# The output products of a head pair dealt over two steps in the second and fourth attention

## The reference

```python
q = (x @ Wq).reshape(B, Nq, h, dh)
k = (context @ Wk).reshape(B, Nk, h, dh)
v = (context @ Wv).reshape(B, Nk, h, dh)
attn = jax.nn.softmax(jnp.einsum('bqhd,bkhd->bhqk', q, k) * scale, axis=-1)
out = jnp.einsum('bhqk,bkhd->bqhd', attn, v).reshape(B, Nq, h * dh)
return out @ Wo + bo
...
x = x + jnp.tanh(g_xattn[1]) * _L1_xattn_ref(_layernorm(x, axis=-1), ctx_768, ...)
```

## Time and profile before

| what | value |
|---|---|
| median of 3 runs | 2148.47 us (2147.4 to 2151.1) |
| profiled execution, its own time | 2147.12 us |
| its span, first to last instruction | 2145.3 us |
| mean granted TensorE clock | 0.900 |
| PE / PEld / DVE / ACT / POOL busy | 82% / 58% / 62% / 59% / 52% |
| second attention | about 347 to 608 us |
| fourth attention | about 1767 to 2028 us |

### The profile page before, as it was taken

The page is one execution under the profiler, slowest core; times in us unless marked ns, Lnnn a source line. Parts: engine busy times, 40 slices in busy tenths (PEclk is TensorE's granted clock), DMA queues, the critical chain, the costliest instruction groups (busy, mean ns, idle before and its releaser), DMA issues. The chain is left out here.

```text
span 2145.3 us, 55182 instructions
## 1 busy us (share of the span) xinstructions
PE 1769.2 (82%) x22168; PEld 1236.0 (58%) x22169; DVE 1329.7 (62%) x2556; ACT 1272.8 (59%) x1627; POOL 1109.8 (52%) x1052
## 2 busy tenths in 40 slices
PE   1699636999947769999999999999736839999778
PEld 1244325888845626666666666666535727888645
DVE  3767376888864366555555555555244547888765
ACT  3357423777734326777777777777624527777553
POOL 2100003555542337777777777777752336775534
PEclk9779858999968859999999999999957969999899
DMA  6401100000032010000000000000122111000000
GB/s 175 80 6 11 27 0 2 3 3 3 2 102 74 25 47 11 11 14 11 10 13 12 11 10 14 11 10 11 32 83 56 36 48 34 3 3 3 2 6 16
DMA packets 95263, 55.20 MB, mean 26 GB/s; under 512 B 43341, under 2 KB 88728, under 8 KB 94918
## 3 DMA queue, kind: packets, MB, share of 16 engines
q1 hardware_dynamic: 86820, 42.61, 8.2%
q0 software_dynamic: 3584, 6.36, 0.9%
q10 hardware_dynamic: 4610, 2.71, 0.5%
HBM read 30.16 MB, written 13.75 MB: 20 GB/s over the span
## 5 line engine op out<-in xcount | busy, mean ns | idle before, releaser
L1422 POOL TENSOR_TENSOR aw_p_lo<-aw_p,aw_p_hi 128x512 f16<-128x512 f32 x512 | 576.5, 1158 | 191.0 <-issue 168.8
L1438 DVE TENSOR_REDUCE aw_max_part<-ps 128x1 f32<-128x512 f32 x512 | 351.2, 690 | 289.7 <-PE ps L1244 284.9
L859 POOL TENSOR_TENSOR ap_p_lo<-ap_p,ap_p_hi 128x512 f16<-128x512 f32 x256 | 291.0, 1158 | 181.6 <-issue 173.9
L1374 ACT ACTIVATE aw_p<-ps 128x1024 f32<-128x1024 f32 x256 | 260.0, 1015 | 206.1 <-PE ps L1275 204.0
L1289 PE MATMUL ps<-ctx_hi_lo,aw_p_hi 128*128 128x97 f16 x2048 | 288.9, 206 | 2.5 <-POOL aw_p_lo L1422 2.5
L1291 PE MATMUL ps<-ctx_hi_lo,aw_p_hi 128*128 128x96 f16 x2048 | 288.0, 207 | 0.0
L1293 PE MATMUL ps<-ctx_hi_lo,aw_p_lo 128*128 128x97 f16 x2048 | 287.4, 204 | 0.0
L1381 ACT ACTIVATE aw_p_hi<-aw_p 128x1024 f16<-128x1024 f32 x256 | 270.6, 1057 | 8.1
L1291 PEld LDWEIGHTS ps<-ctx_hi_lo,aw_p_hi 128*128 128x128 f16 x2048 | 197.9, 97 | 25.2
L1289 PEld LDWEIGHTS ps<-ctx_hi_lo,aw_p_hi 128*128 128x128 f16 x2048 | 196.5, 96 | 12.1 <-POOL aw_p_lo L1422 4.7
L1293 PEld LDWEIGHTS ps<-ctx_hi_lo,aw_p_lo 128*128 128x128 f16 x2048 | 201.9, 99 | 0.0
(11 more groups left out here) (464 smaller groups left out, 4979.8 us busy)
## 6 DMA issues: line engine op xcount, KB each, us to landing
sf_weights_raw<-in_L_w SPq DMA_DIRECT2D x24, 256.0 KB, 4.2
slot_scratch<-at_empty_rows SPq DMA_DIRECT2D x16, 260.0 KB
sf_fetched<-slot_scratch SPq DMA_DIRECT2D x16, 260.0 KB, 2.9
sf_weights_raw<-in_L_w SPq DMA_DIRECT2D x8, 512.0 KB, 3.9
x_norm<-result_scratch SPq DMA_DIRECT2D x8, 256.0 KB, 4.0
aw_queries<-aw_queries SPq DMA_DIRECT2D x32, 64.0 KB, 1.9
aw_queries<-aw_q_lo SPq DMA_DIRECT2D x32, 64.0 KB, 2.0
raw<-in_L_q SPq DMA_DIRECT2D x3, 512.0 KB, 11.9
```

The costliest lines, as they stand in the source:

```text
L859: nc.gpsimd.tensor_tensor(p_lo[:, i % 2, h, :], p[:, i % 2, h, :], p_hi[:, i % 2, h, :], ALU.subtract).then_inc(lo_done, 1)
L1374: nc.scalar.activation(p[:, n % 2, :].rearrange("p (b q) -> p b q", b=2), s, ACT.Exp, scale=1.0 / QS).then_inc(exp_done, 1)
L1422: nc.gpsimd.tensor_tensor(p_lo[:, n % 4, cols], p[:, n % 2, cols], p_hi[:, n % 4, cols], ALU.subtract).then_inc(lo_done, 1)
L1438: nc.vector.tensor_reduce(mpart[:, b % 2, k:k + 1], ps[:, max_bank(b, k), :], AX.X, ALU.max).then_inc(m_done, 1)
```

## The change

`project(u)` becomes `project(u, half)`. It is called in every step instead of in every second one: in the odd step `2u + 3` with half 0 (query tiles 0 and 1, six products), in the even step `2u + 4` with half 1 (query tiles 2 and 3, six products). Its place inside the step stays, ahead of `weighted(i)`; in an even step that is behind `turn`. The semaphore `y_ready` is raised at the end of half 1 only. The waits at the head of `project` are issued in both calls. `add` goes from the odd to the next even step on VectorE, behind the low half of the turned output and ahead of `max_rows`. The list of steps has one step more at its end.

```diff
-        steps = range(-3, NH + 2)
+        steps = range(-3, NH + 3)
...
-                def project(u):
+                def project(u, half):
                     qb, pair = block_of(u)
                     cols = slice(pair * P, (pair + 1) * P)
                     pe.wait_ge(t_done, u + 1)
                     if pair == 0 and qb:
                         pe.wait_ge(y_done, qb)
-                    for t in range(TQ):
+                    for t in (2 * half, 2 * half + 1):
...
-                    ins.then_inc(y_ready, 1)
+                    if half:
+                        ins.then_inc(y_ready, 1)
...
-                    if i % 2 and is_unit((i - 3) // 2):
-                        project((i - 3) // 2)
+                    if is_unit((i - 3) // 2):
+                        project((i - 3) // 2, 1 - i % 2)
...
-                    if i % 2 and is_unit((i - 3) // 2) and (i - 3) // 2 % NP == NP - 1:
-                        add((i - 3) // 2 // NP)
+                    if i % 2 == 0 and is_unit(i // 2 - 2) and (i // 2 - 2) % NP == NP - 1:
+                        add((i // 2 - 2) // NP)
```

## The result

The changed kernel takes 2135.6 us (median of 5 runs, 2132.26 to 2138.92), the kernel before 2151.1 (5 runs beside it, 2147.4 to 2152.76): ratio 0.9929, 95% interval 0.9912 to 0.9946, so 15 us or 0.7% faster. In a second set of runs it was 2127.74 (6 runs) against 2148.29 (11 runs): ratio 0.9913, interval 0.9887 to 0.9938. Forecast was a gain of 16.8 us, a ratio of 0.9922. The profiled execution took 2135.6 us, its span is 2133.8, and the granted clock is 0.90 as before.

The account below looks back on a forecast made before the run. TensorE bounds odd steps, VectorE even ones. Per attention 8.7 us saved by products plus 1.7, less 2.0 for the add, is 8.4; both give 16.8, so 2131.7 us, range 2128.5 to 2138.

Parts of the forecast that it names:

- What bounds each step: Both attention stretches: TensorE holds odd steps, VectorE even ones; six products leaving cut odd steps from 4.087 to 3.753 us.
- Rival B: Odd steps are not TensorE's, so only the add's move counts: 2.6 us slower, 2151.1; chance 0.03.
- The cover of the even step: Even steps: 0.39 us between TensorE's next free slot and VectorE's release hides the six added products (0.334 us).
- Rival A: Even step's cover is only 0.23 us, or the second wait costs a slot: 2137.8 us; chance 0.09, its extreme 0.02.
- The satisfied wait: Even steps: the repeated wait for the turned rest (t_done) costs nothing, at most one slot of 0.056 us.
- GpSimd and the second head: Even steps: no new TensorE wait for GpSimd; in the fourth attention about 0.03 of 0.36 us is left.
- The add: Residual add moved, three times per attention: odd step without it 4.32 to 4.09, even step plus 0.66 us.
- The ends: Last steps of each attention: no saving in step 61, added products hidden in step 62, no cost in the tail.
- The sum: Both attentions: 8.4 us saved in each, 16.8 us in all.
- C: TensorE loses its clock in the attention, some 3.6 us more per step hit: 2152 us or more; chance 0.02.
- the allowance for the rest of the kernel: Stages behind the attentions, at a changing clock: half the 3.7 us spread of three runs allowed either way.
- the main forecast: Whole kernel: 2131.7 us, its own range 2128.5 to 2134.5; chance 0.80.

Follow-up runs that it names:

- the tile experiments: Changed kernel with its query tiles divided three odd, one even (2134.65 us) or one odd, three even (2134.54 us), instead of two and two.
- one against three: Changed kernel with one query tile's products in the odd step and three in the even: 2134.54 us in one execution.
- three against one: Changed kernel with three query tiles' products in the odd step and one in the even: 2134.65 us in one execution.

## Why the prediction was right

**What bounds each step**: right. Odd steps fell from 4.09 to 3.75, as six products of 0.0557 us say, and tiles added or taken go 0.167 each until VectorE's copy is the bound, at 3.66 (the prediction's 0.11 of room puts it at 3.64). Rival B needed odd steps at 4.09. The Trainium skill (Perfetto Trace Analysis, Identifying the Most-Contended Engine) judges TensorE's headroom by MFU (its arithmetic against the peak), which was not worked out here, and by the busy share of the weight loads; by that share the odd step would be a tenth idle. This case does not agree: the weight loads were busy 3.69 of 4.10, and the step gave back 0.334 for 0.334 of products. For which engine holds a step, the release of its last group told more than that share.

**The cover of the even step**: right, and the choice between readings was the one that mattered. Taken by starts it was 0.39 us; the tile experiments give 0.40. The idle figures of the profile (0.23 of TensorE, 0.51 of the weight load) are off on either side, since the first counts from the end of the last score product (446.89 + 0.27 = 447.16), behind the next free slot at 447.00, and the second from the end of its weight load, ahead of that slot. Rival A, built on 0.23, would have had even steps of 3.69; they are 3.59. The satisfied wait that the even step has now (t_done) costs nothing that shows: the even steps of both tile experiments carry it, and their 0.40 is no less than the 0.39 read from the kernel before, whose even steps had none.

**GpSimd and the second head**: TensorE has no wait for GpSimd in either stretch, and nothing in the odd or even steps grew. In the fourth attention the 0.36 us that GpSimd had left behind its splits is 0.02 now; the forecast was 0.03.

**The add**: 0.66 us more in the even step (4.25) and 0.23 less in the odd one, both as forecast, and moved alone it costs 1.30 per attention.

**The ends**: no saving in step 61 (3.72 before, 3.73 after in the second attention; 3.44 and 3.44 in the fourth), as forecast. The tail was forecast at no cost, and that was wrong in three of four tails. From the last exponential to the last block's add the kernel before takes 9.71 to 9.75 us in its four tails, the changed kernel 10.20 and 10.14 in the first trace, 10.50 and 9.75 in the second. The transposes of the last output in the second attention, before and after, and the windows around them:

```profile
603.99 0.66 PE L960 MATMUL ps<-ident,ap_o 128*128 128x128 f32 x4 [0.73 <-DVE ap_o L1058]
604.00:604.50 0.50, 0.50 (x4) 0.40 (x4) 0.00 (x0) 0.00 (x0) 0.00 (x0) 1.00 0.00 0
```

```profile
594.27 1.12 PE L960 MATMUL ps<-ident,ap_o 128*128 128x128 f32 x4 [0.74 <-DVE ap_o L1059]
594.60:595.50 0.90, 0.90 (x8) 0.84 (x7) 0.00 (x0) 0.08 (x1) 0.00 (x0) 0.50 0.00 0
```

The granted clock falls to 0.50 while they run, where in the kernel before it was still 1.00. With six products instead of twelve in step 63 TensorE waits 1.08 us for GpSimd behind them instead of 0.76. Whether that wait brings the clock down earlier isn't shown: the short tail of the changed kernel has it too.

**The sum**: 16.8 forecast, 16.93 in the steps of the first traces; 15.5 between the medians of the first set of runs, 18.7 by the ratio of the second (0.0087 x 2148.29). The intervals of both sets (11.6 to 18.9 us and 13.3 to 24.3) hold it. The tails' 0.9 us in the first trace are not in these 16.93. C did not come about: the granted clock is 1.00 over both stretches. What was sized too small is the allowance for the rest of the kernel. I took 3.7 us from three runs; the stretch between the attentions alone varies by 12 over ten traces, and the changed kernel's second median (2127.74) lies below the low end given, with the kernel before lower too (2148.29 against 2151.1). The range held for the runs that it was made for, and in part by luck: their median, 2135.6, lies above the 2134.5 that the main forecast allowed itself, in the part of the range that was there for rival A, and A did not come about.

## What to carry to other kernels

In a written-out software pipeline, look for the releaser of the group that closes each kind of step; where one kind is held by TensorE and the other by another engine, divide an accumulation so that part of it lies in the second kind, behind whatever that kind's own chain needs first. Measure the cover by starts (next free slot to release), and check how far each kind of step is from its next bound: with two tiles each these were 0.11 and 0.06 us, so one against three was no better (214.68 against 214.76 us for the 29 pairs) and three against one worse (219.66). A piece of work that moves along with it, here the add, should be priced in its new place: on the chain that sets the step it cost the 0.66 us by which it delayed what follows, and on engines with idle time there, nothing.

## What the runs showed of the hardware

Steps of 3.6 and 4.1 us repeated to 0.01 us from one execution to the next, while the same instructions between the attentions took 1173.5 to 1185.6 us; so here a change inside a regular stage is read far more sharply from the distances inside it than from the time of the whole. ScalarE's copy of a 128x512 bank to 32 bits with a per-partition scale took 0.69 us where the 16-bit copies of such a bank took 0.59 to 0.60, and GpSimd's 32-bit add of the same size 1.27 against 1.16 for its subtraction to 16 bits. A product of 128 columns cost TensorE's stream 0.056 us at a granted clock of 1.00 and 0.11 at 0.50, and the weight loads beside such products were busy 90% of a step that had no slack at all.
